# Attention one: row-maximum scores as 64-row products, two heads at a time in the two halves of the array

## The reference, cut to what matters

```python
h = _L0_tok_ref(x, L0_tok_W)                       # (8, 1024, 256)
h = h + _L0_attn_ref(_layernorm(h), Wqkv, bqkv, Wr, br)

def _L0_attn_ref(x, Wqkv, bqkv, Wr, br):
    xh = x.reshape(b, c, h, he).transpose(0, 2, 1, 3)
    qkv = jnp.einsum('bhce,ef->bhcf', xh, Wqkv) + bqkv
    q, k, v = jnp.split(qkv, 3, axis=-1)
    att = jnp.einsum('bhqe,bhke->bhqk', q, k) / jnp.sqrt(jnp.float32(he))
    mask = jnp.tril(jnp.ones((c, c), dtype=att.dtype), k=-1)
    att = jax.nn.softmax(att * mask, axis=-1)
    out = jnp.einsum('bhqk,bhke->bhqe', att, v)
    out = out.transpose(0, 2, 1, 3).reshape(b, c, d)
    return out @ Wr + br
```

## Time and profile before

| | |
|---|---|
| Runs | 2967.66, 2971.22, 2972.97 us; median 2971.22 |
| Profiled execution | 2968.36 us |
| Its span | 2966.6 us, mean granted clock 0.937 |
| PE | 2663.4 us busy, 90% |
| DVE | 2124.2 us, 72% |
| ACT | 1592.2 us, 54% |
| POOL | 1763.9 us, 59% |
| Attention one | from the start to about 1520 us |
| One half in the loop | 88.8 us, window 0 about 50.5 and window 1 about 38.3 |

### The profile page before, as it was taken

The page is one execution under the profiler, slowest core; times in us unless marked ns, Lnnn a source line. Parts: engine busy times, 40 slices in busy tenths (PEclk is TensorE's granted clock), DMA queues, the critical chain, the costliest instruction groups (busy, mean ns, idle before and its releaser), DMA issues. The chain is left out here.

```text
span 2966.6 us, 60258 instructions
## 1 busy us (share of the span) xinstructions
PE 2663.4 (90%) x14742; PEld 1606.7 (54%) x14742; DVE 2124.2 (72%) x5796; ACT 1592.2 (54%) x3630; POOL 1763.9 (59%) x3268
## 2 busy tenths in 40 slices
PE   3788999988999998999876999999999979999999
PEld 1344444444444444444444666666666646676666
DVE  4567676766666767766636999999999965555654
ACT  1455566666566656566531565555656534444444
POOL 3774445444445444445343888778878757777675
PEclk8789999999999989999976999999999979999999
DMA  2343132233133233232240000000000000000000
GB/s 41 82 83 44 23 42 35 30 43 43 23 42 36 28 43 41 24 43 34 31 139 0 1 1 0 0 0 0 0 0 0 1 4 15 16 16 14 16 16 19
DMA packets 60127, 79.13 MB, mean 27 GB/s; under 512 B 20364, under 2 KB 32408, under 8 KB 59416
## 3 DMA queue, kind: packets, MB, share of 16 engines
q1 hardware_dynamic: 55240, 67.74, 16.3%
q0 software_dynamic: 3072, 8.39, 0.9%
q10 hardware_dynamic: 1744, 2.16, 0.2%
HBM read 18.98 MB, written 8.39 MB: 9 GB/s over the span
## 5 line engine op out<-in xcount | busy, mean ns | idle before, releaser
L463 ACT ACTIVATE probs<-scoresT 128x512 f32<-128x512 f32 (+3 forms) x1536 | 695.6, 491 | 499.4 <-PE scoresT L601 490.8
L551 DVE TENSOR_REDUCE cand<-ring 128x4 f32<-128x512 f32 x1152 | 730.0, 682 | 193.3 <-PE ring L653 170.9
L384 POOL TENSOR_SCALAR_AFFINE_SELECT probs<-probs 128x128 f32<-128x128 f32 x1024 | 293.2, 294 | 524.6 <-ACT probs L463 520.0
L601 PE MATMUL scoresT<-stage 98*128 98x512 bf16 (+3 forms) x1536 | 490.6, 361 | 75.4 <-ACT probs L463 63.7
L653 PE MATMUL ring<-stage 96*128 96x512 bf16 (+2 forms) x1792 | 421.8, 311 | 19.3 <-DMA stage<-parts 14.3
L615 PE MATMUL pv<-probs,Vg 128*32 128x512 f32 (+3 forms) x3072 | 318.1, 519 | 3.1 <-POOL probs L384 3.0
L601 PEld LDWEIGHTS scoresT<-stage 98*128 98x128 bf16 x1536 | 146.4, 100 | 280.8 <-ACT probs L463 220.2
L653 PEld LDWEIGHTS ring<-stage 96*128 96x128 bf16 x1792 | 161.6, 99 | 224.6 <-DVE cand L551 94.2
L1075 PE MATMUL mm<-w_W,x2T 128*128 128x512 f32 x512 | 244.3, 600 | 0.0
L1055 PE MATMUL mm<-w_W,hT 128*128 128x256 f32 x1024 | 243.4, 381 | 0.0
L1136 ACT ACTIVATE hT<-mmT,w_be,w_g 128x128 f32<-128x128 f32 x512 | 185.5, 469 | 77.4 <-PE mmT L1066 77.4
(11 more groups left out here) (256 smaller groups left out, 5432.4 us busy)
## 6 DMA issues: line engine op xcount, KB each, us to landing
stage<-parts SPq DMA_DIRECT2D x256, 96.0 KB
stage<-parts SPq DMA_DIRECT2D x256, 64.0 KB
stage<-parts SPq DMA_DIRECT2D x256, 32.0 KB
out<-result SPq DMA_DIRECT2D x64, 128.0 KB, 1.7
stage<-ct SPq DMA_DIRECT2D x128, 4.0 KB
w_W<-in_W SPq DMA_DIRECT2D x4, 512.0 KB
h<-in_WT,tok POOLq DMA_INDIRECT x64, 2.8
stage<-in_tok_ SPq DMA_DIRECT2D x1, 1024.0 KB, 4.9
```

The costliest lines, as they stand in the source:

```text
L384: nc.gpsimd.affine_select(out=d, in_=d, compare_op=ALU.is_gt, fill=0.0, base=0, pattern=[[1, P]], channel_multiplier=-1).then_inc(mask_ok, 1)
L463: nc.scalar.activation(probs[:, n % 8, lo:hi], scoresT[u % SCORE_BANKS][:, lo % 512:(hi - 1) % 512 + 1], ACT.Exp, scale=SOFT).then_inc(exp ...
L551: ins = nc.vector.tensor_reduce(c, src[:].rearrange("p (t a b) -> p t a b", t=c.shape[1], b=P), AX.X, ALU.max)
L601: nc.tensor.matmul(scoresT[u % SCORE_BANKS][:, lo % 512:(hi - 1) % 512 + 1], Ks[0:ROWS, gi, hh, P * kt:P * kt + P], Qs[0:ROWS, gi, hh, lo: ...
```

## The change

MX no longer reads the stacks Qs and Ks. It gets its own, `Qm` and `Km`: 64 rows a head (the products of the two upper parts with the two upper parts), two heads on top of each other in 128 partitions, for two pairs of heads. For each bank number, PE fills the banks of both heads of a pair with products in the upper and the lower 64 rows of the array; the mask needs two products a head, since an identity of 128 rows does not fit into 64. There is one set of Qm and Km, not two: the transfers of the group after next (`LOAD_MAX`, 4 a pair) are issued as soon as a pair's maxima are final. In "init" they follow the LOAD (`LOAD_FIRST`). MAX_FINAL, CT and their transfers go by pairs.

The core of the diff:

```diff
         at(pos_of["LOAD"], ("LOAD",))
+        if not scores:
+            at(pos_of["LOAD"], *(("LOAD_FIRST", p) for p in range(PAIRS_MX)))
         uses = []
-        for h in range(HPG):
+        for p in range(PAIRS_MX):
             for k in range(MAX_BANKS):
-                uses.append([("R", "MX", "dve", h, k)])
-                if h and k == 1:
-                    uses[-1].append(("MAX_FINAL", h - 1))
-                if h and k == 5:
-                    uses[-1].append(("R", "CT", "dve", h - 1))
-        uses.append([("MAX_FINAL", HPG - 1), ("R", "CT", "dve", HPG - 1), ("EQ",)])
+                uses.append([("R", "MX", "dve", 2 * p, k), ("R", "MX", "dve", 2 * p + 1, k)])
+                if p and k == 3:
+                    uses[-1] += [("R", "CT", "dve", p - 1)]
+                if p and k == 4 and load_max:
+                    uses[-1] += [("LOAD_MAX", p - 1)]
+            uses[-1] += [("MAX_FINAL", p)]
+        uses.append([("R", "CT", "dve", PAIRS_MX - 1), ("EQ",)] + ([("LOAD_MAX", PAIRS_MX - 1)] if load_max else []))
 ...
+                sp.wait_ge(const_ok, 3)
+                for j in range(2):
+                    for i in range(2):
+                        rows, half = slice(HALF * j, HALF * j + HALF), slice(HALF * i, HALF * i + HALF)
+                        sp.dma_start(ident2[rows, i, :], ident_b[half, :]).then_inc(w_in, 16)
+                        sp.dma_start(future2[rows, i, :], future[half, :]).then_inc(w_in, 16)
 ...
                         if e[1] == "LOAD":
-                            sp.wait_ge(parts_ok, 4 * (hb + 1 + e[0]))
-                            wait(sp, st_ok, UNITS * (g - 1))
+                            if section == "loop":
+                                wait_apart(sp, (parts_ok, 4 * (hb + 1 + e[0])), (st_ok, UNITS * (g - 1) + 2 * HPG))
+                            else:
+                                sp.wait_ge(parts_ok, 4 * (hb + 1 + e[0]))
+                                wait(sp, st_ok, UNITS * (g - 1) + 2 * HPG)
 ...
+                        elif e[1] in ("LOAD_FIRST", "LOAD_MAX"):
+                            p, first = e[2], e[1] == "LOAD_FIRST"
+                            if first:
+                                wait_apart(sp, (parts_ok, 4 * (hb + 2)))
+                            else:
+                                wait_apart(sp, (parts_ok, 4 * (hb + 2)), (m_ok, PAIRS_MX * g + p + 1))
+                            lo = 16 * (HPG * (par if first else 1 - par) + 2 * p)
+                            rows = slice(lo, lo + 32)
+                            for i in range(2):
+                                sp.dma_start(Qm[i:P:2, p, :], parts[rows, 0, i:i + 1, :].broadcast_to([32, 2, S])).then_inc(max_in[p], 16)
+                                sp.dma_start(Km[i:P:2, p, :], parts[rows, 1, 0:2, :]).then_inc(max_in[p], 16)
 ...
                                 if w == 0 and c == 0:
                                     act.wait_ge(w_in, 16 * WEIGHTS)
                                     for s in stack_in:
-                                        wait(act, s, 96 * 2 * (hb + 1))
+                                        wait(act, s, 16 * 12 * 2 * (hb + 1))
+                                    for s in max_in:
+                                        wait(act, s, 16 * 4 * 2 * (hb + 1))
 ...
-                            if kt == 0:
-                                pe.wait_ge(shift_in[hh], 16 * (G + 1))
+                            if kt == 0 and hh % 2 == 0:
+                                pe.wait_ge(stack_in[hh // 2], 16 * 12 * (G + 1))
+                                pe.wait_ge(shift_in[hh // 2], 16 * 2 * (G + 1))
 ...
+                            def mask(at, n, start, stop):
+                                for i in range(2):
+                                    for j in range(2):
+                                        ins = nc.tensor.matmul(out[j][:, P * at:P * (at + n)], ident2[half[j], i, :],
+                                                               future2[half[j], i:i + 1, :].broadcast_to([HALF, n, P]),
+                                                               start=start and i == 0, stop=stop and i == 1,
+                                                               tile_position=(half[j].start, 0))
 ...
+                                for x in range(2):
+                                    ins = nc.tensor.matmul(out[x][:, P * at:P * (at + n)], Qm[half[x], hh // 2, P * i:P * i + P],
+                                                           Km[half[x], hh // 2, P * j:P * (j + n)], start=not every, stop=stop,
+                                                           tile_position=(half[x].start, 0))
```

More of the change, by code:

```diff
@@ L30 @@
 ROWS = STACK + 2
+PAIRS_MX = HPG // 2
+HALF = P // 2
 MAX_PLAN = [
@@ L86, with window @@
          "WR": 14, "VG": 14, "LOAD": 14, "MX": 15, "MX_END": 31, "MX_CURVE": 1.0}
-def window(gi, ot, wr, tail, prologue, v, scores, following):
+def window(gi, ot, wr, tail, prologue, v, scores, following, load_max=False):
     others = {}
@@ L161, in plan @@
     sections = {
-        "init": window(1, False, False, False, True, True, False, True),
-        "first": window(0, False, False, False, True, not v1, True, True) + window(1, False, False, True, False, v1, True, True),
-        "loop": window(0, True, not wr1, True, True, not v1, True, True) + window(1, False, wr1, True, False, v1, True, True),
+        "init": window(1, False, False, False, True, True, False, True, True),
+        "first": window(0, False, False, False, True, not v1, True, True, True) + window(1, False, False, True, False, v1, True, True, True),
+        "loop": window(0, True, not wr1, True, True, not v1, True, True, True) + window(1, False, wr1, True, False, v1, True, True, True),
         "last": window(0, True, not wr1, True, False, False, True, True) + window(1, False, wr1, True, False, False, True, False),
@@ L212, in attention_one @@
                   for n in range(2))
+        Qm, Km = sb("Qm", [P, PAIRS_MX, S], BF16), sb("Km", [P, PAIRS_MX, S], BF16)
         Vg = sb("Vg", [P, 2, TPB, HPG, 32])
@@ L240, in attention_one @@
         vg_ok = sem("vg_ok")
-        stack_in = [sem(f"stack_in{i}") for i in range(HPG)]
-        shift_in = [sem(f"shift_in{i}") for i in range(HPG)]
+        stack_in = [sem(f"stack_in{i}") for i in range(PAIRS_MX)]
+        shift_in = [sem(f"shift_in{i}") for i in range(PAIRS_MX)]
+        max_in = [sem(f"max_in{i}") for i in range(PAIRS_MX)]
         m_ok, cm_c, cm_ok, eq_ok = sem("m_ok"), sem("cm_c"), sem("cm_ok"), sem("eq_ok")
@@ L548, in run @@
                                 hh, k = e[4:6]
+                                if k == 0:
+                                    wait(dve, m_ok, PAIRS_MX * g + hh // 2)
                                 tiles, cols = MAX_PLAN[k][2]
@@ L618, in run @@
                             ins.then_inc(pv_ok, 1)
+                        elif kind == "R" and e[2] == "MX":
+                            hh, k = e[4:6]
+                            if hh % 2:
+                                continue
+                            pair = e, [x for x in plans[section] if x[:4] == e[:4] and x[4:6] == (hh + 1, k)][0]
+                            if k == 0:
+                                pe.wait_ge(max_in[hh // 2], 16 * 4 * (g + 1))
+                            for x in pair:
+                                bank_free(pe, section, num, x)
+                            out = [ring[x[-1][0] % RING_BANKS] for x in pair]
+                            half = [slice(HALF * i, HALF * i + HALF) for i in range(2)]
+                            runs, diagonal, _ = MAX_PLAN[k]
+                            every = diagonal == (0, 4)
+                            def mask(at, n, start, stop):
+                                for i in range(2):
+                                    for j in range(2):
[3 more added lines that the diff above has]
+                                                               tile_position=(half[j].start, 0))
+                                        if stop and i == 1 and at + n == 4:
+                                            ins.then_inc(filled, 1)
+                            if every:
+                                mask(0, 4, True, False)
+                            at = 0
+                            for i, j, n in runs:
+                                masked = not every and diagonal == (at + n - 1, 1)
+                                stop = at + n == 4 if every else not masked
+                                for x in range(2):
+                                    ins = nc.tensor.matmul(out[x][:, P * at:P * (at + n)], Qm[half[x], hh // 2, P * i:P * i + P],
+                                                           Km[half[x], hh // 2, P * j:P * (j + n)], start=not every, stop=stop,
+                                                           tile_position=(half[x].start, 0))
+                                    if at + n == 4 and stop:
```

(7 more changed lines are left out.)

60 lines of the change are left out of this document (21 added, 39 removed).

## The result

The changed kernel takes 3222.51 us (median of 4 runs, 3220.01 to 3227.03), the kernel before 2971.87 in the same session: a ratio of 1.0848, 95% interval 1.0829 to 1.0867. The forecast was 3062 with a range up to 3125. The sign was right. Of the 251 us, 91 had been forecast.

What follows compares the result with a forecast made beforehand. PE was taken to bound both windows of attention one. Against 2968.4 us: wait 72 + clock 36 - pairs 30 - last half 1 + "init" 14 = +91, giving 3059, as median 3062; range 2985 to 3125.

Steps and rivals of the forecast that it cites:

- What the pairs bring: Products of head pairs in both windows, after mode changes: 2.0 us less a half, 30 us in 15 halves.
- what of it reaches the end: Gain left after waits and DVE's limit: about 1.0 us in window 0 and 1.0 in window 1 of each half.
- the lumpier order: Window 1, two banks at once out of four: PE's gain of 1.2 us counted as 1.0.
- Costed at nothing: Constant transfers, 8 more transfers a group on SP, half as many MAX_FINAL and CT; PE's last-maximum wait stays as now.
- The wait: Window 0: the later LOAD delays ACT's QK, so PE waits 4.8 us at the second SUF; 72 us in 15 halves.
- The clock after that wait: Window 0, behind PE's new wait: lower granted clock loses 2.4 us a half, 36 us in 15 halves.
- Window 1: The late LOAD makes nothing wait there; DVE allows 4 us, PE gives 1.2, of which 1.0 counted as gain.
- The products and the mode changes: Overlapping row halves save 3.96 us a window; 28 mode changes at 0.10 cost 2.8, so 1.2 remain.
- init: At the start: the first MX product needs the LOAD and four more transfers, so everything moves 14 us later.
- Behind attention one: Stages after attention one: no cost of their own; they only shift with attention one's end.
- all moves one for one: A change in attention one, the first 1520 us of 2966.6, moves everything behind it by the same amount.
- the third: Rival: the array's halves do not overlap, small products run one after another; +264 us, 3235 us, chance 0.09.

Runs made afterwards that it cites:

- e5: a1 with the own stacks loaded first in "init" and ten one-column DVE memsets ahead of the MoE loop: 3057.53 us, ratio 1.0301.
- e6: Kernel before with the order by pairs but its 96-row products from the old stacks, no own stacks, early LOAD, ten DVE memsets: 3071.39 us, ratio 1.0338.
- after: The changed kernel itself, against the kernel before: 3222.51 us, ratio 1.0848.
- e12: e9 with the late LOAD of the changed kernel: 3080.36 us, ratio 1.0378.
- e10: Kernel before with six products that nobody reads ahead of each half's last CT: 2951.05 us, ratio 0.9931.
- e9: e5 with nine products that nobody reads put into the last CT's bank ahead of its wait: 3011.13 us, ratio 1.0132.
- a1: Changed kernel without the later LOAD, with one semaphore for each parity of the stacks: 3107.97 us, ratio 1.0483.
- a4: Kernel before with eight 32 KB transfers behind window 0's LOAD, which ACT's first QK waits for: 3064.77 us, ratio 1.0330.
- e7: e6 with the own stacks' transfers of the change, which nothing reads: 3141.57 us, ratio 1.0573.
- a3: Changed kernel with the LOAD early as in a1 and products and masks over all 128 rows instead of two halves: 3093.22 us, ratio 1.0419.
- e8: Kernel before with twelve DVE instructions fewer ahead of the MoE loop, same work: 2995.49 us, ratio 1.0076.
- e11: e5 with the last CT at position 30 of window 0 (was 27) and 28 of window 1 (was 26): 3031.00 us, ratio 1.0196.

## Why the prediction was wrong

A half was to grow by 4.8 + 2.4 - 2.0 = 5.2 us and grew by 13.3. Over 15 halves these 8.1 are 121 of the 160 us that the forecast lacks; 43 more lie behind attention one. By its own steps:

- **What the pairs bring.** This is the step that failed most: -2.0 us a half ("what of it reaches the end"). With the late LOAD taken out the half is still 5.1 us longer than before (e5), so the term is wrong by 7.1, in sign too. The order by pairs alone does it: 5.1 a half (e6), where the forecast had taken 0.2 off window 1's 1.2 for the lumpier order. The traces show where: PE waits 2.8 us a half for DVE to read ring banks, where it was 0.1 in before; the last CT of window 1 waits 2.54 us and not 1.55, since it stands behind the reductions of two heads' banks; and PE is 1.6 us longer busy, at a clock of 0.88 instead of 0.93 (e5). The argument looked at DVE's busy time, 4 us below PE's in window 1, and concluded that DVE would not bind. It did not look at when a bank comes free.
- **Costed at nothing: the last maximum, and its clock.** "Still has PE waiting, as now." Filling that wait in the loop of the changed kernel takes 5.1 us off a half (after to e12, which differ otherwise in the loop by semaphores alone), in before 1.2 (e10): 3.9 of the 13.3 hang on it. Also costed at nothing were the own stacks' transfers on SP, which delay the LOAD (e9).
- **The wait.** Right in place and near in size: 4.8 forecast, 4.55 read.
- **The clock after that wait.** 2.4 forecast. Wait and clock together were 7.2, and measured 8.2 (a1 to after), or 5.1 when the other pause is filled (e9 to e12); in the old kernel the clock of such a pause came to 3.4 (a4). The term is near for the pause that it prices. What was wrong is that each pause was priced by itself. At the low clock a half has 6.8 us during and behind the LOAD's wait, 6.9 behind the last CT of window 0, 3.5 within window 1, and 14.5 behind its last CT; before has 6.8 and 3.4.
- **Window 1.** Forecast -1.0, measured +6.0. e12 has it at +1.2 when PE does not idle at the window's end.
- **The products and the mode changes.** Each price was right (0.22 us for a pair, 0.10 each way for the mode). Their net, forecast as a gain, is a gain of some 0.9 by e7 against e5, and none by a1 against a3, neither clear of the spread of halves. The Trainium skill, TensorEngine Tiling (Array Packing), Theoretical Speedup, allows up to 2x for a contraction of at most 64 rows. The trace agrees for a pair by itself, and the time of a half does not show it.
- **What the pairs cost beside pauses.** With the last CT's wait filled in both kernels the pairs still cost 4.3 us a half (92.2 in e9, 87.9 in e10), at nearly the same missing clock (3.5 and 3.0). PE waits there 2.8 us for DVE and 2.1 at the second SUF, and in e10 0.1 and nothing. How much of the 4.3 each of the two makes was not tested.
- **"init".** Right: +14 forecast, +15.7 measured, all given back when the own stacks go first (e5).
- **Behind attention one.** Forecast nothing, measured +43 us. It goes with the place of DVE's code in the MoE stage (e5, e8). Nothing in the argument looked past the end of the changed stage, beyond the sentence that all moves one for one.

The sum now, by the runs: 15 halves at 13.3 (8.2 of late LOAD with its clock, 5.1 of the pairs) are 199, with 16 in "init" and 43 behind it 258; the span grew by 253.6. The 13.3 can also be read as 5.1 of late LOAD, 4.3 of pairs and 3.9 of the empty wait. Of the rivals, the third (halves that do not overlap) came near the time, 3235, by coincidence: a pair's products do overlap, as the trace of the changed kernel shows.

What stays open: why a DVE loop of 306 instructions stalls when it starts at its engine's 1218th or 1216th instruction and not at the 1228th. These three places, counted in instructions and not in addresses, are all that was tried. Nor was it followed up what makes one execution's halves short or long (a1, a3, e5), or the split between steady and outer halves in e9 and e11.

## What to carry to other kernels

Price an idle stretch of TensorE not by its length but by it and the half-clock stretch behind it, and look where the change lengthens *existing* pauses: two waits in one half did not simply add up. Where work is made lumpier, as here with two banks at once out of a ring of four, compare when each bank comes free, not busy times. A pause that can't be removed can be filled with products that nobody reads; here that paid in the kernel before as well. And compare the stages that a change does not touch: the instruction count alone moved one of them by 24 to 43 us.

## What the runs showed of the hardware that I had not expected

- With 10 or 12 instructions fewer on DVE ahead of a hardware loop, each of its 11 jumps back costs one or two stalls of 2.0 to 2.7 us, with 95 packets on the instruction queue in place of 40; adding ten brought it back to 41 (after, e8, e5).
- Nine more products in each last CT's wait (2.54 and 1.83 us) raised the granted clock of the halves shown from 0.89 to 0.96, and in before six raised it from 0.94 to 0.96 (e9, e10).
- With fewer columns to stream, the row halves of a1 ran at 0.88, where the full-array products of a3 ran at 0.92 (means over 13 halves), in about the same time.
- Two products in the two row halves of the array overlap fully: 0.22 us for the pair of 512 columns.
